# Routing one-hots: the product with the entry's number made by GpSimd instead of VectorE

## The reference

```
logits = jnp.einsum('bsd,de->bse', xn, Wr) + br
top_vals, top_idx = jax.lax.top_k(logits, K)          # K = 2, E = 8
w = jax.nn.softmax(top_vals, axis=-1)
w_full = jnp.einsum('bsk,bske->bse', w, jax.nn.one_hot(top_idx, E, dtype=w.dtype))
for e in range(E):
    h = gelu(xn @ W1[e] + b1[e])
    y = y + (h @ W2[e] + b2[e]) * w_full[..., e, None]
```

## Time and profile before

| what | before |
|---|---|
| median of three runs | 4126.31 us |
| the profiled execution, its own time | 4131.88 us |
| span of the profiled execution | 4130.1 us |
| the part of `route` ahead of the chunks | 3220.6 to 3255.1 |
| the 28 chunks, to the end of the last L2348 | 3255.1 to 3303.84 |
| from there to the first matmul of `experts` | 3303.84 to 3313.0 |

### The profile page before, as it was taken

The page is one execution under the profiler, slowest core; times in us unless marked ns, Lnnn a source line. Parts: engine busy times, 40 slices in busy tenths (PEclk is TensorE's granted clock), DMA queues, the critical chain, the costliest instruction groups (busy, mean ns, idle before and its releaser), DMA issues. The chain is left out here.

```text
span 4130.1 us, 75106 instructions
## 1 busy us (share of the span) xinstructions
PE 3336.9 (81%) x20075; PEld 2432.6 (59%) x20075; DVE 2912.6 (71%) x7656; ACT 1435.7 (35%) x4413; POOL 2813.7 (68%) x2528
## 2 busy tenths in 40 slices
PE   7677777444888888888888888888888499999995
PEld 6455545343444444444445666666666489999994
DVE  8899999785666666666656666666666855555587
ACT  2355555353111111111102333333333345555542
POOL 0388888663777777777777777777777056666674
PEclk9688887655899999999968999999999799999998
DMA  2111111386444444444434554554544322222367
GB/s 82 18 3 3 3 3 3 64 273 207 126 125 125 125 126 124 123 125 126 128 101 124 151 152 151 152 151 151 150 149 147 103 64 70 70 71 70 121 248 258
DMA packets 283329, 471.48 MB, mean 114 GB/s; under 512 B 94311, under 2 KB 180076, under 8 KB 283247
## 3 DMA queue, kind: packets, MB, share of 16 engines
q0 software_dynamic: 139776, 272.64, 25.1%
q1 hardware_dynamic: 131423, 189.44, 13.5%
q10 hardware_dynamic: 12050, 8.45, 0.6%
HBM read 349.06 MB, written 122.65 MB: 114 GB/s over the span
## 5 line engine op out<-in xcount | busy, mean ns | idle before, releaser
L1638 POOL DMA_INDIRECT rows<-table,idx x1664 | 1671.0, 1004 | 507.9 <-issue 429.8
L2086 PE MATMUL ps_seg<-rows,pick 128*128 128x256 f32 x3328 | 1056.8, 423 | 344.5 <-DMA rows<-table,idx 333.6
L1921 DVE TENSOR_TENSOR acc<-acc,ps_seg 128x256 f32 x1664 | 698.0, 419 | 612.9 <-PE ps_seg L2086 501.3
L2086 PEld LDWEIGHTS ps_seg<-rows,pick 128*128 128x128 f32 x3328 | 572.3, 196 | 751.4 <-DMA rows<-table,idx 637.0
L771 POOL DMA_INDIRECT records<-sort_rec,sort_addr x280 | 528.3, 1887 | 260.0 <-DVE sort_rec L874 157.7
L1763 DVE TENSOR_SCALAR pick<-iota_row,loc,ewt 128x128 f32<-128x128 f32 x1680 | 522.0, 363 | 3.9
L2548 POOL DMA_INDIRECT y_rows<-arena,spot x204 | 290.3, 1423 | 200.8 <-DVE idx L2603 126.9
L2690 PE MATMUL ps_h<-arena,up_now 128*128 128x128 f32 x3264 | 401.3, 277 | 5.2 <-ACT arena L2564 3.0
L926 PE MATMUL ps_out<-acc 128*128 128x240 bf16 x1568 | 277.9, 361 | 144.7 <-DVE acc L860 144.5
L2690 PEld LDWEIGHTS ps_h<-arena,up_now 128*128 128x128 f32 x3264 | 382.8, 193 | 7.9 <-issue 4.3
L2674 PE MATMUL ps_y<-down_now,arena 128*128 128x256 f32 x1632 | 386.0, 380 | 0.0
(11 more groups left out here) (396 smaller groups left out, 4825.9 us busy)
## 6 DMA issues: line engine op xcount, KB each, us to landing
rows<-table,idx POOLq DMA_INDIRECT x1664, 2.8
acc<-y_rows SPq DMA_DIRECT2D x20, 896.0 KB
xn<-xn_dram SPq DMA_DIRECT2D x100, 128.0 KB, 2.2
xT_dram<-xT SPq DMA_DIRECT2D x98, 128.0 KB
xn<-xT_dram SPq DMA_DIRECT2D x49, 256.0 KB, 3.6
skip<-skip_dram SPq DMA_DIRECT2D x49, 256.0 KB, 3.9
x_rows<-acc SPq DMA_DIRECT2D x49, 256.0 KB, 2.6
ffn_rows<-kv SPq DMA_DIRECT2D x49, 256.0 KB, 2.3
```

What stands on the lines that cost most here:

```text
L1638: pool.indirect_dma_start(out=rows[:, t, :], out_offset=None, in_=k.table, in_offset=bass.IndirectOffsetOnAxis(idx[:, h, t:t + 1], 0), bou ...
L1921: dve.tensor_tensor(here, here, sums(u), ALU.add).then_inc(added[u], 1)
L2086: last = pe.matmul(sums(t), pick[:, h, t, :], rows[:, t, :], start=True, stop=True)
```

## The change

The multiplication that makes `at_lane_entry` is taken out of VectorE's list and put in GpSimd's, with the same operands and in the same 28 pieces. GpSimd waits for `routed` 5 (the constants that VectorE has cast), for `placed` (the buffer of two chunks before is free) and for `lane_made`. VectorE gets one wait more: before it overwrites `at_lane` of chunk n it waits until `entry_weighted` has reached n - 1, which is to say until GpSimd has read the one of chunk n - 2. Two small functions for views are shared between the engines.

```
+                pool.wait_ge(routed, 5)
+                for n, (f, at) in enumerate(CHUNKS_P):
+                    by_lane, of_entries = views(n % 2, at)
+                    start_after(pool, placed, n - 1)
+                    pool.wait_ge(lane_made, n + 1)
+                    pool.tensor_tensor(by_lane(at_lane_entry), by_lane(at_lane), of_entries(entry2, wide),
+                                       ALU.mult).then_inc(entry_weighted, 1)
...
                     start_after(dve, row_weighted, n - 1)
+                    start_after(dve, entry_weighted, n - 1)
                     dve.tensor_tensor(by_lane(at_lane), twos(lane_no[:, :]).unsqueeze(1).to_broadcast(wide),
                                       of_entries(lane2, wide), ALU.is_equal).then_inc(lane_made, 1)
...
-                    dve.wait_ge(lane_made, n + 1)
-                    dve.tensor_tensor(by_lane(at_lane_entry), by_lane(at_lane), of_entries(entry2, wide),
-                                      ALU.mult).then_inc(entry_weighted, 1)
```

More of the change, by code:

```diff
@@ L2201, in route, with views @@
         twos = lambda a: a.rearrange("p (n two) -> p n two", two=2)
+        wide = [P, FEW, P // 2, 2]
+        def views(m, at):
+            return (lambda t: t[:, m, :, :].rearrange("p b (l two) -> p b l two", two=2),
+                    lambda t, shape: t[:, at:at + FEW, :].unsqueeze(2).to_broadcast(shape))
         with nc.Block() as block:
@@ L2334, in _ @@
                     m, (start, end) = n % 2, SPANS[f]
-                    wide = [P, FEW, P // 2, 2]
                     narrow = [P, FEW, (end - start) // 2, 2]
-                    by_lane = lambda t: t[:, m, :, :].rearrange("p b (l two) -> p b l two", two=2)
-                    of_entries = lambda t, shape: t[:, at:at + FEW, :].unsqueeze(2).to_broadcast(shape)
+                    by_lane, of_entries = views(m, at)
                     start_after(dve, row_weighted, n - 1)
+                    start_after(dve, entry_weighted, n - 1)
                     dve.tensor_tensor(by_lane(at_lane), twos(lane_no[:, :]).unsqueeze(1).to_broadcast(wide),
```

## The result

The changed kernel takes 4158.89 us (median of 4153.78 to 4159.16, three runs) against 4126.31: 1.0068 times as long, with an interval of 1.0054 to 1.0081, or 22 to 33 us. It is slower, as forecast, by less than the 41 us forecast. The profiled execution after took 4159.16 us with a span of 4157.4, which is 27.3 over the span before. That is the difference to explain; the medians are 5 us further apart because the profiled execution of before was itself 5.6 above its median.

A forecast was written before the change was run, and what follows sets the result against it. VectorE was taken to set the pace of the 28 uncovered chunks (48.74 us); GpSimd's 58.0 plus 31.8 of VectorE's time make 89.8, +41.1, so 4126.3 + 41 = 4167 us, 1.0% slower, range 4134 to 4200.

The forecast's parts named there:

- The place and the sign: 28 chunks of `route`: VectorE sets their pace, each us they gain or lose moves the end; slower was given 0.85.
- The two engines in each other's way: Chunks: GpSimd and VectorE exclude each other when both read two things from SBUF; times add, chance 0.64.
- A: Experiments' theory for the chunks: VectorE and GpSimd exclude each other when both read two things from SBUF; their times add.
- B: Experiments' theory for the chunks: no exclusion; the product takes 2.00 by itself, and at_lane's 2.10 holds a wait.
- The rival of overlap: Chunks: VectorE's short instructions slip between, GpSimd alone sets the pace; +9.9 us, 4136; chance 0.18.
- the two others: Chunks: faster, engines overlap and product 1.1 us, 4112, chance 0.05; much slower, broadcast product 4.0 us, 4223, chance 0.13.
- The length of the product: Each chunk's product of 896 numbers on GpSimd: 2.07 us, 28 of them 58.0 us.
- The lower bound: Product on GpSimd at 1.63 ns per number, from one-input line 1126 (256 numbers in 554 ns): 1.60 us.
- The share that adds: Chunks: 0.95 of the 33.5 us of at_lane and at_tile adds to GpSimd's time, 31.8 us (26.5 to 33.5).
- The waits: Chunks: VectorE's added wait on entry_weighted and GpSimd's on `placed` cost nothing beyond the sum.
- The end: Last seven matmuls after the chunks: TensorE may have a lower clock, 0 to 0.8 us more, put at nothing.

The follow-up runs named there:

- half: Changed kernel, but GpSimd makes the product of the 14 even chunks only and VectorE that of the 14 odd ones; 1.0040 of the kernel before, chunks 62.05 us.
- split: Changed kernel, but in each chunk GpSimd multiplies 4 of the 7 entries and VectorE 3; 1.0043 of the kernel before, chunks 64.9 us.
- psum: Changed kernel with the rulers lane_no and tile_no as f32 in PSUM instead of bf16 in SBUF; 1.0038 of the kernel before, chunks 63.6 us.
- psum_lane: Changed kernel with only the ruler lane_no moved to PSUM; 4143.33 us against 4127.22 for the kernel before, chunks 61.5 us.
- probe: Kernel before plus one GpSimd instruction of seven kinds in turn per chunk, for which VectorE waits; 4502.48 us against 4463.17.
- serial: Changed kernel with two more waits, so the product runs beside nothing on VectorE; 4182.72 us against 4127.22 for the kernel before, chunks 90.8 us.
- beside_two: Kernel before plus seven GpSimd instructions of 896 bf16 (broadcast, flat, one input) beside the chunks, for which nobody waits; 4144.66 us against 4128.93.
- beside: Kernel before plus GpSimd memsets, one-input and two-input multiplications beside some chunks, for which nobody waits; 4153.28 us against 4127.22.

## Why the prediction was right, and where it was off

**The place and the sign** were right. VectorE sets the pace of the chunks, nothing covers them, and what they lose the end loses: 26.7 us in the chunks, 27.3 in the span. "The two engines in each other's way" was right too: the chunks of `half`, `split`, `psum` and `psum_lane` each came within 4.1 us of what A had forecast for them, and about 11 us or more from B. The rival of overlap (4136) is refuted by `half`, and the two others by `probe`: the product is neither under 1.1 us nor near 4. A chunk took 2.63 in the first part, where the prediction had 3.2 on average; both terms of the sum were too high, as follows.

**The length of the product** is the term of the sum that was most mis-sized: 2.07 us forecast, 1.685 measured undisturbed. It makes 28 x 0.385 = 10.8 of the 14.4 us by which the stretch came out shorter (75.4 for 89.8). I had two points, 98 numbers at 348 ns and an iota of two numbers at 137, and drew the line through both. But the iota is another kind of instruction with a lower fixed part; `probe` puts that of a two-input one at 0.186, and 49 ns too little at the foot of a line through 98 numbers became 0.39 us at 896. The lower bound, 1.60 from line 1126, was nearer, by luck: `probe` shows one-input instructions on another line again (2.46 for 896). The estimate of 1.97 from the Trainium skill's "GPSIMD Engine Reference", section 3.1, was off by nearly as much.

**The share that adds** was 0.95 of VectorE's 33.5 us, 31.8. Measured: 75.44 less 28 x 1.685 = 47.2 leaves 28.3, a share of 0.84, between the 0.79 of the earlier trace rows and the 0.95 of the earlier trace rows. This is the other 3.5 us, and the 1.00 at the top of the range was too high by 5.2. `split` and `half` fit one reading of the rest: the fixed 0.19 of each product lies beside VectorE's work, 28 x 0.19 = 5.2.

**The waits** cost nothing beyond the sum, as forecast: 75.44 is reached to 0.1 us with no term for them. `serial`, which has them one step tighter, takes 90.8.

**The end.** 0 to 0.8 us for a lower clock of TensorE was not seen: the mean granted clock in the chunks fell from 0.93 to 0.59, with TensorE idle for 20.6 of the 75.44 us where it had been for 15.8 of 48.74, but the last seven matmuls, in the timeline after, took 0.79 against 0.78:

```profile
3330.45 0.79 PE L2411 MATMUL ps_entry<-acc 128*128 128x204 bf16 x7 [0.41 <-POOL acc L2263]
```

The prediction had TensorE at under 1.2 us for a chunk throughout. With the lower clock it took 54.86 / 28 = 1.96 on average. That was still less than the chunk's 2.63, so GpSimd's wait for `placed` cost nothing, with less room than forecast.

**The time.** 4167 lies 8 us above 4158.89, and the forecast loss of 41 compares with 27.3 in the spans and 32.6 in the medians. The medians flatter the sum: by the trace it was too long by 14.

## To carry to other kernels

Here the move of elementwise work from VectorE to GpSimd took nothing off a full VectorE whose instructions have two inputs in SBUF: the product cost VectorE 0.54 us before and shut it out for 1.50 after. The move won its 15 us only where the VectorE instructions beside it had one input in PSUM, and these were themselves so much slower that the whole was still slower than the kernel before. One input in SBUF is no safe sign either, as the TENSOR_SCALAR of `beside_two` shows (1.68 for 0.27). So before such a move, count not what each engine is busy but what both have to read, and try one pair of the instructions in question side by side. And price an instruction that the trace does not have from two lengths of its own kind, not from one length and another kind's fixed part.

## What was not expected of the hardware

- A GpSimd instruction that reads SBUF stood for 37.8 us (`beside`) and 42.25 us (`beside_two`) beside a VectorE queue of two-input instructions without gaps, 20 chunks and more of three each, though in the changed kernel the same kind got its turn within 0.53 us every time (1.997 to 2.212 for 1.685). A memset of the same size took its 0.84 beside the same queue.
- On GpSimd a multiplication by a constant, one input, took 2.46 us for 896 bf16 numbers and one with two inputs 1.68; bf16 and f32 cost the same per number (934 ns for 448 of either), and so did a broadcast and a flat operand (1685 and 1681).
- A VectorE instruction with one input in SBUF and none in PSUM, a TENSOR_SCALAR of 128x204 f32, took 1.68 us for 0.27 beside a two-input product of GpSimd.
